# Two chunks of the middle of a feed-forward net share one PSUM bank, in a new order of stages

## What is computed

```
x = layernorm(x + L0(x, adj))      # graph attention, ELU
x = layernorm(x + L1(x, adj))      # three layers L1.0, L1.1, L1.2:
      scores = leaky_relu(x@a1 + (x@a2).T + b), masked, softmax
      h = layernorm(x + attn @ x)
      x = layernorm(h + gelu(h @ W1[l] + b1[l]) @ W2[l] + b2[l])   # 256 -> 1024 -> 256
x = layernorm(x + L2(x, adj))      # graph attention, only the top 16 weights of a row kept, ELU
x = layernorm(x + L3(x, adj))      # 8-head attention, ReLU, projection
```

## Time and profile before

| | |
|---|---|
| median of three runs | 3801.18 us (3792.32 to 3809.88) |
| the profiled execution | 3815.43 us, its span 3813.8 us |
| TensorE, matmuls | busy 3324.7 us, 87% of the span |
| VectorE | 2460.1 us, 65% |
| ScalarE | 2204.2 us, 58% |
| GpSimd | 773.0 us, 20% |
| mean granted TensorE clock | 0.961 |

### The profile page before, as it was taken

One profiled execution on the slowest core, in us unless ns is written; L12 is line 12 of the kernel. 1 busy time (PEld: TensorE's weight loads), 2 busy tenths in 40 slices (PEclk: granted clock), 3 DMA queues, 4 the chain that ended last, 5 costly groups with the idle time before them and its releaser, 6 DMA issues.

```text
span 3813.8 us, 59841 instructions
## 1 busy us (share of the span) xinstructions
PE 3324.7 (87%) x18048; PEld 2558.3 (67%) x18048; DVE 2460.1 (65%) x7151; ACT 2204.2 (58%) x4349; POOL 773.0 (20%) x1052
## 2 busy tenths in 40 slices
PE   6689989898898899889998898989989898899866
PEld 4576766767667676666766677676766766667653
DVE  3466676666757666676666767666676666767654
ACT  3256556665565756656665575756656665565623
POOL 1212122121211222121121212122121121211210
PEclk8899999999999999999999999999999999999988
DMA  5000000000000000000000000000000000000000
GB/s 137 1 1 12 7 12 7 7 7 7 12 7 10 3 7 12 7 12 7 7 7 7 12 7 12 1 7 12 7 12 7 7 6 7 12 7 1 1 6 6
DMA packets 39858, 40.24 MB, mean 11 GB/s; under 512 B 7264, under 2 KB 38240, under 8 KB 39520
## 3 DMA queue, kind: packets, MB, share of 16 engines
q1 hardware_dynamic: 31072, 27.68, 2.4%
q0 software_dynamic: 8448, 8.39, 1.5%
HBM read 36.07 MB, written 8.39 MB: 12 GB/s over the span
## 4 chain that ended last, share of the span: by engine, by line
PE 48%; issue 25%; ACT 11%; DVE 11%; POOL 4%; DVEq 0%; DMA 0%; POOLq 0%; ACTq 0%; SPq 0%
PE acc L1187 11%; PE work L1209 9%; PE acc L1223 7%; PE acc L1289 3%; PE work L1130 3%; ACT PT L1036 3%; PE acc L1258 3%; POOL rstd L510 2%; PE acc L1270 2%; PE acc L1318 2%; PE work L1103 2%; PE work L1238 2%; ACT L1036 2%; PE work L1173 1%; DVE stats L759 1%
## 5 line engine op out<-in xcount | busy, mean ns | idle before, releaser
L1209 PE MATMUL work<-XT,w_sb 128*128 128x256 f32 x3072 | 732.7, 384 | 36.7 <-DVE XT L816 15.0
L510 POOL TENSOR_TENSOR rstd<-var_eps,minus_half 128x2 f32<-128x2 f32 x320 | 225.1, 703 | 2641.4 <-DVE var_eps L768 2641.2
L1223 PE MATMUL acc<-w_sb,gT 128*128 128x256 f32 x3072 | 731.4, 385 | 0.0
L1209 PEld LDWEIGHTS work<-XT,w_sb 128*128 128x128 f32 x3072 | 557.6, 190 | 168.2 <-ACT gT L1018 35.5
L1223 PEld LDWEIGHTS acc<-w_sb,gT 128*128 128x128 f32 x3072 | 579.9, 193 | 97.8 <-issue 22.8
L1018 ACT ACTIVATE gT<-work,b_sb 128x256 f32<-128x256 f32 x768 | 343.1, 473 | 208.6 <-PE work L1209 201.1
L1187 PE MATMUL acc<-X,PT 128*128 128x256 f32 x1536 | 387.6, 410 | 24.8 <-ACT PT L986 24.2
L1187 PEld LDWEIGHTS acc<-X,PT 128*128 128x128 f32 x1536 | 312.7, 207 | 108.8 <-issue 46.3
L1018 ACT ACT_TABLE_LOAD x198 | 254.0, 1283 | 3.5
L752 DVE COPY PT<-work 128x512 f32<-128x512 f32 x160 | 109.5, 684 | 225.5 <-PE work L1173 223.8
L759 DVE BATCH_NORM_STATS2 stats<-R 128x6 f32<-128x256 f32 x640 | 240.9, 418 | 11.0
(11 more groups left out here) (153 smaller groups left out, 5934.7 us busy)
## 6 DMA issues: line engine op xcount, KB each, us to landing
HX<-in_x SPq DMA_DIRECT2D x16, 512.0 KB, 3.8
pos<-in_adj POOLq DMA_DIRECT2D x16, 512.0 KB, 5.7
out<-X SPq DMA_DIRECT2D x32, 256.0 KB, 2.1
w_sb<-in_L_gnn_W SPq DMA_DIRECT2D x6, 1024.0 KB, 8.4
g_sb<-in_L_gnn_g SPq DMA_DIRECT2D x6, 128.0 KB, 6.7
awr_sb<-in_L_gnn_attn_w SPq DMA_DIRECT2D x2, 256.0 KB, 7.9
c_sb<-in_L_gnn_beta SPq DMA_DIRECT2D x3, 128.0 KB, 4.5
PT<-in_L_gnn_b SPq DMA_DIRECT2D x3, 128.0 KB, 5.7
```

Of the source, the lines that this page charges most:

```text
L510: pool.tensor_tensor(rstd[s][:, half_rows(half)], var_eps[s][:, half_rows(half)], minus_half[:], ALU.pow)\
L1209: last = pe.matmul(u.bank[:, 0:HN], w1_sb[:, l, c, f * P:(f + 1) * P], XT[s][:, c, half * HN:(half + 1) * HN], start=(c == 0), stop=(c == ...
L1223: last = pe.matmul(acc[s][half][:, i, :], gT[s][:, f, i * P:(i + 1) * P], w2_sb[:, l, f, :], start=(f == 0 and i == 0), stop=(f == FC - 1) ...
```

## The change

It does three things.

1. In `uses`, a quarter of the net's first matmul is one use instead of two. TensorE waits once for a bank and writes both chunks, each 256 columns wide, side by side; one `filled` is given behind the second. ScalarE waits once and runs two Gelu activations, one for each half of the bank.
2. The first Gelu of a pair raises a new semaphore, `chunk_read`, the second raises `evacuated`. The second matmul, which takes the chunks one by one, waits for `chunk_read` before the even chunk and for `evacuated` before the odd one.
3. `HALF` is another order of the same 296 stages.

```diff
-        ("middle", "L0", "v1"), ("ending", "L1.2", "hT0 ha0 sum1 norm1 f100 f101 hT1"),
-        ("middle", "L0", "bc zs0"), ("ending", "L1.2", "ha1"), ("middle", "L0", "mx0"),
-        ("ending", "L1.2", "f102"), ("middle", "L0", "zs1"), ("ending", "L1.2", "f103"),
-        ("middle", "L0", "exp0 mx1"), ("ending", "L1.2", "f200"), ("middle", "L0", "exp1 pT0 pT1"),
-        ("ending", "L1.2", "f110"), ("middle", "L0", "agg0"), ("ending", "L1.2", "f201 f111"),
-        ("middle", "L0", "pT2 pT3 sum0"), ("ending", "L1.2", "f202 f112 f203"), ("middle", "L0", "norm0 agg1"),
-        ("ending", "L1.2", "f113 xsum0 xnorm0"), ("middle", "L1.0", "xT0"), ("middle", "L0", "sum1"),
-        ("ending", "L1", "norm0"), ("ending", "L1.2", "f210 f211"), ("middle", "L0", "norm1"),
-        ("ending", "L2", "xT0"), ("middle", "L1.0", "xT1"), ("ending", "L2", "v0"), ("middle", "L1.0", "s bc"),
-        ("ending", "L1.2", "f212"), ("middle", "L1.0", "zs0 mx0 zs1 exp0 mx1 exp1"),
-        ("ending", "L1.2", "f213 xsum1"), ("middle", "L1.0", "pT0 pT1"), ("ending", "L1.2", "xnorm1"),
-        ("ending", "L1", "norm1"), ("middle", "L1.0", "agg0 pT2 pT3"), ("ending", "L2", "xT1 v1"),
-        ("middle", "L1.0", "sum0 norm0 agg1 hT0 ha0 sum1"), ("ending", "L2", "bc zs0 mx0"),
...
+        ("middle", "L0", "v1"), ("ending", "L1.2", "hT0 ha0"), ("middle", "L0", "bc"),
+        ("ending", "L1.2", "sum1 norm1 f100 f101 hT1"), ("middle", "L0", "zs0 mx0"), ("ending", "L1.2", "ha1"),
+        ("middle", "L0", "zs1"), ("ending", "L1.2", "f102 f103"), ("middle", "L0", "exp0 mx1 exp1"),
+        ("ending", "L1.2", "f200"), ("middle", "L0", "pT0"), ("ending", "L1.2", "f110"),
+        ("middle", "L0", "pT1 agg0 pT2 pT3 sum0"),
+        ("ending", "L1.2", "f201 f111 f202 f112 f203 f113 xsum0 xnorm0"), ("middle", "L0", "norm0"),
+        ("ending", "L1", "norm0"), ("middle", "L0", "agg1"), ("middle", "L1.0", "xT0"),
+        ("middle", "L0", "sum1 norm1"), ("ending", "L1.2", "f210 f211"), ("ending", "L2", "xT0"),
+        ("middle", "L1.0", "xT1 s bc zs0 mx0 zs1"), ("ending", "L2", "v0"), ("middle", "L1.0", "exp0 mx1"),
+        ("ending", "L1.2", "f212 f213"), ("middle", "L1.0", "exp1 pT0"), ("ending", "L1.2", "xsum1"),
+        ("middle", "L1.0", "pT1"), ("ending", "L1.2", "xnorm1"), ("middle", "L1.0", "agg0"),
+        ("ending", "L1", "norm1"), ("middle", "L1.0", "pT2 pT3"), ("ending", "L2", "xT1"),
+        ("middle", "L1.0", "sum0 norm0 agg1 hT0"), ("ending", "L2", "v1 bc zs0"),
+        ("middle", "L1.0", "ha0 sum1"), ("ending", "L2", "mx0"), ("middle", "L1.0", "norm1 f100 f101 hT1"),
+        ("ending", "L2", "zs1"), ("middle", "L1.0", "ha1 f102"), ("ending", "L2", "exp0"),
...
+        ("middle", "L1.1", "bc zs0 mx0"), ("ending", "L3", "v1 qk1"), ("middle", "L1.1", "zs1 exp0 mx1"),
+        ("ending", "L3", "ex0"), ("middle", "L1.1", "exp1 pT0"), ("ending", "L3", "ex1 sq1 ex2 ex3"),
+        ("middle", "L1.1", "pT1 agg0 pT2"), ("ending", "L3", "sr1 uT0 ex4 uT1 ex5 uT2 ex6"),
+        ("middle", "L1.1", "pT3"), ("ending", "L3", "uT3 ex7"), ("middle", "L1.1", "sum0 norm0"),
...
+        ("ending", "L3", "ex11"), ("middle", "L1.1", "norm1"), ("ending", "L3", "sq3"),
+        ("middle", "L1.1", "f100 f101"), ("ending", "L3", "pv0 uT8"), ("middle", "L1.1", "hT1 ha1"),
+        ("ending", "L3", "ex12 pc0 sr3"), ("middle", "L1.1", "f102"), ("ending", "L3", "uT9 ex13 uT10 ex14"),
...
-            uses += [(f"hT0 {k}", DC), (f"g0 {k}", 2 * FQ), (f"hT1 {k}", DC), (f"g0 {k}", FC - 2 * FQ), (f"g1 {k}", FC)]
+            uses += [(f"hT0 {k}", DC), (f"g0 {k}", 2), (f"hT1 {k}", DC), (f"g0 {k}", 2), (f"g1 {k}", 4)]
...
+        chunk_read = signal("chunk_read", [(f"g{h} {k}", 4) for k in L1K for h in range(2)])
...
-                    for f in range(quarter * FQ, (quarter + 1) * FQ):
-                        u = Use(s, it, f"g{half} {key}", f)
-                        act.wait_ge(u.filled, u.turn)
-                        act.activation(gT[s][:, f, :], u.bank[:, 0:HN], ACT.Gelu, bias=b1_sb[:, l, f:f + 1]).then_inc(u.evacuated, 1)
+                    u = Use(s, it, f"g{half} {key}", quarter)
+                    f = quarter * FQ
+                    act.wait_ge(u.filled, u.turn)
+                    act.activation(gT[s][:, f, :], u.bank[:, 0:HN], ACT.Gelu, bias=b1_sb[:, l, f:f + 1])\
+                        .then_inc(chunk_read.sems[s], 1)
+                    act.activation(gT[s][:, f + 1, :], u.bank[:, HN:N], ACT.Gelu, bias=b1_sb[:, l, f + 1:f + 2])\
+                        .then_inc(u.evacuated, 1)
...
-                    for f in range(quarter * FQ, (quarter + 1) * FQ):
-                        u = Use(s, it, f"g{half} {key}", f)
-                        pe.wait_ge(u.evacuated, u.turn)
+                    u = Use(s, it, f"g{half} {key}", quarter)
+                    pe.wait_ge(u.evacuated, u.turn)
+                    for i in range(FQ):
+                        f = quarter * FQ + i
                         for c in range(DC):
-                            last = pe.matmul(u.bank[:, 0:HN], w1_sb[:, l, c, f * P:(f + 1) * P],
+                            last = pe.matmul(u.bank[:, i * HN:(i + 1) * HN], w1_sb[:, l, c, f * P:(f + 1) * P],
                                              XT[s][:, c, half * HN:(half + 1) * HN], start=(c == 0), stop=(c == DC - 1))
-                        last.then_inc(u.filled, 1)
+                    last.then_inc(u.filled, 1)
...
+                        if f % FQ == 0:
+                            pe.wait_ge(chunk_read.sems[s], chunk_read.value(it, f"g{half} {key}", quarter))
+                        else:
+                            pe.wait_ge(u.evacuated, u.turn + 1)
```

More of the change, by code:

```diff
@@ L1218, in stage @@
                         pe.wait_ge(acc_evacuated[half].sems[s], acc_evacuated[half].value(it, key + " ffn") - 1)
+                    u = Use(s, it, f"g{half} {key}", quarter)
                     for f in range(quarter * FQ, (quarter + 1) * FQ):
-                        u = Use(s, it, f"g{half} {key}", f)
-                        pe.wait_ge(u.evacuated, u.turn + 1)
+                        if f % FQ == 0:
+                            pe.wait_ge(chunk_read.sems[s], chunk_read.value(it, f"g{half} {key}", quarter))
+                        else:
+                            pe.wait_ge(u.evacuated, u.turn + 1)
                         for i in range(HT):
```

## The result

The changed kernel takes **3829.3 us** (median; 3826.1 to 3830.3) against 3805.2 us (3792.3 to 3809.9) beside it: ratio **1.0075, interval 1.0055 to 1.0095** (the ratio on record, with its interval; the quotient of the two medians alone is 1.0063). That is inside the range of 3768 to 3840 us, 22 us above the number given, and on the slower side of the line of 0.5%, where the prediction had put 0.27. The profiled execution spans 3827.5 us at a mean granted clock of 0.961; the one of before had 3813.8 us at the same clock. In these two executions the half-rate level takes 301 and 297 us, so nearly all of their difference of 14 us comes from the order and the banks.

The account below looks back on a forecast made before the run. TensorE was taken to bound the kernel, by its work and the stalls in its stage order. Terms 0 - 0.2 + 0.7 = +0.5 us per half, +7 over 15 halves, from 3801 less 1 gave 3807 us; range 3768 to 3840.

Parts of the forecast that it names:

- Part 1: At the f1 stages, the second of two adjacent stages no longer waits for the first's Gelu: -0.8 us per half.
- the sign given: Sign that the forecast is right: f1's weight loads wait under 10 us for gT in all.
- the ceiling of 50.9 us: Whole old trace: waits for Gelu of f1 (35.5 us) and transposes (15.4 us), the most that could be saved.
- Part 2: Shared bank: the Gelu pair ends 0.37 us later, delaying hT1 in L1.2 and L1.0, +0.5; no new f2 wait.
- rival 3: The pair's 0.37 us lateness reaches TensorE at 8 of 24 f1 stages per half: 3834 us; chance 0.08.
- Part 3: Order in L0, L1.0, L2: a new 2.1 us stall at xT0 is regained later; net about 0.
- rival 2: norm0 of L0 behind xnorm0: the 2.1 us at xT0 are not regained, 3832 us; chance 0.19.
- Part 4: L3 with L1.1: agg0 -0.65, sq2 +0.5, f102 +0.4, sq5 -0.45; sum -0.2 us per half.
- Part 5: Half-clock stretch at 934.5 to 939.5 us: xsum1 to f102 come 1.0 later in two of three halves, +0.7.
- 1: Rival: the freed f1 waits count in full and some slow stretches stay away, 3774 us; chance 0.28.
- 4: Rival: bank sharing does nothing, only the order counts, +0.3 per half, 3812 us; chance 0.45 together with the forecast.
- The likeliest case: Whole kernel: same time within about 0.5% (19 us), chance 0.44, against faster 0.29 and slower 0.27.

Follow-up runs that it names:

- e_bank_only: The kernel before with only the shared bank added, keeping the old order of stages; ratio to before 1.0118.
- e_norm0: The changed kernel with norm0 of L0 moved back ahead of f113, xsum0 and xnorm0; ratio to before 1.0144.
- e_front: Shared bank, the new order up to xT1 of L3 and the old order from there; ratio to before 1.0026.
- e_order_only: The changed kernel with a bank for each chunk again, so the new order alone; ratio to before 1.0497.
- e_before_norm0: The kernel before with norm0 of L0 moved behind xsum0 and xnorm0, as the change has it; ratio to before 1.0081.

## Why the prediction was right or wrong

**Part 1, f1's waits.** 11.4 us in all (35.5 before); the sign given was under 10, so it missed narrowly. As a sum for the two orders it held; as a statement of what the sharing is worth it did not: in the new order it saves 153 us, since that order puts Gelus behind exponentials on ScalarE. What was wrong here is the ceiling of 50.9 us, read from the old order's waits.

**Part 2, the pair.** hT1 of L1.2 waits 0.72 us; 0.75 was said. f2 does not show up among the waits for gT. At agg0 of L0, for which the sum had -0.15, the mean of the halves is +0.4, but that is a slow stretch in v1 in some of them; between the quickest halves it is -0.12. So for the new order the part held. For the old one, which e_bank_only has, it did not: the lateness has a second way there, through the exponentials behind the pair on ScalarE (rival 3's spread).

**Part 3, L0 to L2.** xT0 waits 2.09 (2.1), xT1 stands at 931.0 (931.4), agg0 at 942.9 (943.3), xT1 of L2 at 949.5 (949.1), `bc` waits 0.88 (0.9), hT1 of L1.0 stands at 962.3 (962.0 to 962.3). This half begins 0.3 us earlier in the changed kernel's trace, so against its start xT1 of L2 is 0.7 us and hT1 of L1.0 0.3 to 0.6 later than said, the others within 0.2. agg0 of L1.0 is 1.7 us late in the mean, under the 2 that would have spoken for rival 2. At L3 +0.8 in the mean of twelve halves, +0.5 between the quickest halves; parts 3 and 5 together had +0.7. Right, and e_norm0 shows the giving back by itself; what makes it possible, norm0 of L1 waiting on VectorE, was not named.

**Part 4, L3: the step that failed.** It had -0.2 us per half; by time x clock the new L3 part costs 0.4 more than the old one in e_front, which in its turn carries 0.73 at hT1 and sq5: 1.1, so 1.3 too little was counted. Against e_front, with the same stages in front of it, the changed kernel stands 0.1 us later at agg0 of L1.1 (0.3 between the quickest halves), where -0.65 was said: pT0 comes 1.3 us later, and the wait of 1.54 at 1018.94, for ScalarE's copy, takes back most of what sq1 behind it saves. sq2's +0.5 was 0.64. At sq5 the gain was counted and came. The other side of f203's place there, sq6, was not looked at: 1.05 us, 1.27 in the row at 1074.04. The terms at agg0 and sq6, 0.8 and 1.05, make up the miss and more; 0.2 came back between sq3 and sq5, and where the rest did is not placed.

**Part 5, the clock.** +0.7 us per half, 10 us, was said. The changed kernel's time x (1 - clock) is 147 us against 133 in the mean of the runs of before; at 0.76 to 0.85 that is 11 to 12 us. The size is right, the place only in part. Worked out from both traces, mean of twelve halves, the slow level takes 5.4 us ahead of L3 instead of 3.1, which is the side where the part looked; but the stretch at 934 to 939 us stays in most halves as long as it was, 3.4 us, and others come beside it. Behind the start of L3 it takes 6.8 us instead of 8.5, of which the part knew nothing: the stretch at agg0 of L1.1 goes, and the one at proj0 doubles. Changed kernel, then the kernel before:

```profile
1096.00:1100.00 4.00, 3.37 (x8) 2.50 (x8) 4.00 (x12) 3.36 (x8) 0.00 (x0) 0.50 0.00 0
1100.00:1104.00 4.00, 4.00 (x41) 2.12 (x41) 2.46 (x9) 1.81 (x6) 0.00 (x0) 0.72 0.01 4
```

```profile
1096.00:1100.00 4.00, 2.26 (x9) 1.72 (x8) 3.29 (x9) 3.19 (x6) 0.00 (x0) 0.86 0.00 0
1100.00:1104.00 4.00, 4.00 (x41) 2.03 (x40) 3.52 (x12) 2.87 (x9) 0.00 (x0) 0.71 0.02 4
```

8 x (0.50 + 0.28) = 6.2 us in these two pieces against 8 x (0.14 + 0.29) = 3.4. Why the one goes and the other grows was not settled.

**The rivals.** 1 is out: no half is freed. 2 named the size (3832) for the wrong reason: its stall is given back here, and real only in the old order (1.5 us of it). 3 is partly real, 0.4 us at pT0 of L0, in the old order. 4, that the sharing does nothing, is the most wrong of all. The likeliest case, no difference, missed; 3829 lay inside the range only because it reached to rivals 2 and 3, and neither's mechanism made the time: that is luck.

## What to carry to other kernels

Price a buffer change and a reordering together: waits read under the old order bound neither what the buffers are worth under the new one nor what they cost. When a stage is pulled ahead of another, look at what now directly precedes the stage behind it; a gain at one and a loss at the next are often one trade. And where TensorE sets the time and its clock moves, compare time x clock and the clock apart, and part a long wait rather than merely moving it: in the new order the same idle time in one piece of 3.4 us instead of two cost 0.7%. It is no rule for every place: in the old order, moving the same entry cost 1.5 us per half and left the clock as it was.

## What I had not expected of the hardware

The granted clock made as much of most differences as the order did (e_order_only aside). Among kernels with the same matmuls its mean ranged from 0.949 to 0.966; in the profiled executions e_norm0 has 2 x 0.050 x 3868 = 387 us of the slow level and e_before_norm0 2 x 0.034 x 3819 = 260. One edit, norm0's place, moved the mean by 0.009, and another, f212's, by 0.010 back. The slow stretches read here were 3.4 to 10.2 us long, and one gone at agg0 of L1.1 came with a longer one at proj0. The same kernel varies too: the kernel before ran between 0.960 and 0.970, in 3779 to 3817 us.
